# Two triangle-style layers on one core: Newton roots on VectorE, centring and normalising on GpSimd, the fourth contraction among residual steps

## The reference

```python
# layer 0
z_norm = _layer_norm(z, ln_w, ln_b)
a = (z_norm @ W_ap + b_ap) * jax.nn.sigmoid(z_norm @ W_ag + b_ag) * m
b = (z_norm @ W_bp + b_bp) * jax.nn.sigmoid(z_norm @ W_bg + b_bg) * m
out = jnp.einsum('bikc,bkjc->bijc', a, b)
return z + (out @ W_z + b_z)
# layer 1
x = _layernorm(pair_repr, ln1_w, ln1_b)
left = jax.nn.sigmoid(x @ left1) * (x @ left2)
right = jax.nn.sigmoid(x @ right1) * (x @ right2)
p = jnp.einsum('nsre,nkre->nske', left, right)
p = _layernorm(p, ln2_w, ln2_b)
g = jax.nn.sigmoid(jnp.einsum('nsrz,zy->nsry', x, gate))
q = jnp.einsum('nrse,ez->nsrz', p, out_w) * g
return residual + q
```

## Time and profile before

| | us |
|---|---|
| median of 3 runs | 1036.89 |
| lowest and highest | 1032.7, 1040.85 |
| the profiled execution | 1038.49 |
| its span in the trace | 1036.7 |
| mean granted TensorE clock (share of full speed) | 0.953 |

### The profile page before, as it was taken

How to read it: one execution, slowest core, us unless ns; L and a number is a source line. 1 busy time by engine, 2 the same in 40 slices (tenths; PEclk the granted TensorE clock), 3 DMA queues, 4 the chain that set the end, 5 groups by cost and what they waited for, 6 DMA issues and landing times.

```text
span 1036.7 us, 26385 instructions
## 1 busy us (share of the span) xinstructions
PE 832.8 (80%) x9820; PEld 794.4 (77%) x9820; DVE 763.3 (74%) x1851; ACT 635.2 (61%) x866; POOL 587.9 (57%) x409
## 2 busy tenths in 40 slices
PE   0744455576899899989579999998999899989875
PEld 0644445476899898979469999898989898989864
DVE  3799999976669967995592588825981698059796
ACT  0698877764757636753364476635763676256664
POOL 3599998885436604650582144423761467148797
PEclk9999986778999999999899999999999999999989
DMA  2355568998689817968683368874983598777665
GB/s 81 92 164 162 155 206 263 325 333 263 231 271 298 270 42 238 315 219 274 237 249 108 112 207 257 298 279 131 299 265 122 151 303 252 257 248 235 196 227 191
DMA packets 173238, 228.72 MB, mean 221 GB/s; under 512 B 11064, under 2 KB 109624, under 8 KB 171064
## 3 DMA queue, kind: packets, MB, share of 16 engines
q1 hardware_dynamic: 173112, 227.04, 69.2%
HBM read 134.73 MB, written 92.27 MB: 219 GB/s over the span
## 4 chain that ended last, share of the span: by engine, by line
PE 40%; DVE 21%; DMA 16%; issue 12%; ACT 4%; POOL 4%; SPq 3%; DVEq 0%; POOLq 0%; ACTq 0%
PE bank L1052 16%; PE bank L1032 7%; DVE stats L895 6%; DMA xin<-in_x_dram 6%; PE bank L1033 6%; PE ps_w L1082 5%; DVE split L939 4%; DMA chunk<-xcol 3%; DMA chunk<-xt 2%; DVE xc L932 2%; PE ps_t L1067 2%; DVE var L902 2%; DMA xt<-xt 2%; POOL rstd L633 2%; DVE xc L924 2%
## 5 line engine op out<-in xcount | busy, mean ns | idle before, releaser
L633 POOL TENSOR_TENSOR rstd<-var,minus_half 128x8 f32<-128x8 f32 x192 | 341.2, 1778 | 388.2 <-DVE var L902 388.2
L1052 PE MATMUL bank<-rhs,lhs 128*128 128x128 f32 x2048 | 246.7, 281 | 17.0 <-DVE lhs L875 9.2
L1052 PEld LDWEIGHTS bank<-rhs,lhs 128*128 128x128 f32 x2048 | 238.0, 196 | 20.6 <-DVE lhs L875 8.9
L689 ACT ACTIVATE sig<-bank 128x512 f32<-128x512 f32 x256 | 151.6, 601 | 72.2 <-PE bank L1033 69.3
L716 ACT ACTIVATE xt<-ps_x 128x1024 bf16<-128x1024 bf16 x128 | 130.9, 1023 | 61.9 <-PE ps_x L1093 45.9
L1093 PE MATMUL ps_x<-ident_b,split 128*128 128x128 bf16 x1024 | 85.6, 232 | 90.1 <-DVE split L939 89.6
L932 DVE TENSOR_TENSOR xc<-xc,rstd 128x504 f32<-128x504 f32 (+1 forms) x192 | 139.2, 725 | 23.0 <-POOL xc L647 19.8
L1093 PEld LDWEIGHTS ps_x<-ident_b,split 128*128 128x128 bf16 x1024 | 67.1, 103 | 103.0 <-DVE split L939 102.1
L1032 PE MATMUL bank<-w_rhs,chunk 128*128 128x128 bf16 x1024 | 135.2, 227 | 8.2 <-DVE rhs L867 3.3
L1032 PE MATMUL bank<-w_lhs,chunk 128*128 128x128 bf16 x928 | 131.4, 234 | 6.7 <-DVE lhs L867 4.4
L1082 PE MATMUL ps_w<-w_out,opair 128*128 128x128 f32 x896 | 124.2, 283 | 13.4 <-ACT opair L708 13.0
(11 more groups left out here) (97 smaller groups left out, 1441.6 us busy)
## 6 DMA issues: line engine op xcount, KB each, us to landing
chunk<-xt SPq DMA_DIRECT2D x90, 512.0 KB, 4.5
xt<-xt SPq DMA_DIRECT2D x80, 512.0 KB, 5.2
xin<-in_x_dram SPq DMA_DIRECT2D x128, 256.0 KB, 4.5
x<-xin SPq DMA_DIRECT2D x64, 256.0 KB, 5.0
xin<-x SPq DMA_DIRECT2D x64, 256.0 KB, 4.7
out_dram<-xin SPq DMA_DIRECT2D x64, 256.0 KB, 4.6
spill<-lhs SPq DMA_DIRECT2D x8, 1024.0 KB, 4.9
chunk<-xcol SPq DMA_DIRECT2D x16, 512.0 KB, 5.9
```

The lines of the kernel that those rows point to most:

```text
L633: g.tensor_tensor(rstd[:, m % 2], var[:, m % 2], minus_half[:, :], ALU.pow).then_inc(rooted, 1)
L689: a.activation(sig[:, s], v[:, 0:C, :], ACT.Sigmoid).then_inc(gated, 1)
L1052: last = mm(bank[:, n], operand["lhs"][:, kh, c, :], operand["rhs"][:, kh, c, :], start=kh == 0, stop=kh == HALVES - 1)
```

## The change

- **Roots.** `variance` and GpSimd's `root` go. For each pair of steps VectorE forms the inverse roots of 16 variances a partition by an integer guess and Newton's method in nine instructions, which `root_in_gap` places one by one between its other instructions. `stats` has four buffers. For z steps the roots are written to a PSUM tensor, for the others to SBUF. The factor 1.5 that the guess leaves out goes into the weights (`ROOT_FACTOR`).
- **Engines.** GpSimd centres all z and x steps and normalises all x and p steps; VectorE normalises the z steps and centres the p steps. GpSimd masks one half of the operands of contractions 1 and 2, beginning four ticks ahead of them; VectorE masks the other (512 elements a unit, one unit ahead).
- **Lags.** Centring and what follows run later: an x step centres at lag 5 (before: 4), its transpose at 7 (6), with steps every other tick at 8 and 10 (5, 7); z steps store at 5 (4), p steps at 5 (4), with their statistics at -2 (-1).
- **Fourth contraction.** The 16 ticks of x steps alone and the 16 of contraction 3 become 16 ticks with one x step and one unit each. The result of contraction 3 goes to the lhs operand's memory, and layer 1's first lhs half to `quad`; the w_out for these steps has its rows interleaved (`w_pairs`).
- **Start.** SyncE issues four x loads, then only the six loads of the first weight set; seven others at tick 1, the diagonal ones at tick 3; ScalarE issues ten. The other sets are prepared at ticks 7 to 9.

```diff
-Z_LAGS = dict(load=-2, stats=0, variance=0, root=0, centre=1, norm=1, high=1, low=2, turn_x=2, xt=3,
-              col=3, store=4, project=3, gates=4, make=5)
+Z_LAGS = dict(load=-2, stats=0, centre=1, norm=2, high=2, low=3, turn_x=3, xt=4,
+              col=4, store=5, project=4, gates=5, make=6)
+X_LAGS = dict(turn=0, turn_out=0, mix=1, load=1, add=2, keep=3, stats=3, centre=5,
+              norm=5, high=5, low=6, turn_x=7, xt=7, store=8, project=0, gates=0, make=1)
+P_LAGS = dict(stats=-2, centre=0, norm=1, turn=1, turn_out=2, mix=2, spread=-1,
+              gate=1, gate_out=3, scale=3, load=3, residual=4, store=5, gate_load=-3, project=0, gates=1, make=1)
...
     for n in range(STEPS):
-        tick("x alone", X_BASE + 2 * STEPS + n)
-    contraction(3)
+        tick("x in contraction", X_BASE + 2 * STEPS + n, unit=(3, n))
...
+NORM_EARLY, NORM_LATE = 0, 4 * STEPS
+OTHERS_AT = 7
...
 def centre_on_pool(m):
-    return m < Z_EARLY or Z_LATE <= m < P_BASE
+    return m < P_BASE
+
+def norm_on_pool(m):
+    return m < NORM_EARLY or m >= NORM_LATE
...
+        def roots_of(pair):
+            if OTHERS_AT + 5 <= 2 * pair and not norm_on_pool(2 * pair):
+                return ps_w[:, pair % 2, 0:2 * COLS].rearrange("p (s t) -> p s t", s=2)
+            return rstd[:, pair % 2]
...
-            for m in range(2):
+            for m in range(RING):
                 load_x(m)
-            for dst, src in loads:
-                sp.dma_start(dst, src).then_inc(loaded, 16)
+            for dst, src in first_loads:
+                sp.dma_start(dst, src).then_inc(first_loaded, 16)
...
             for t in range(T_END):
-                for m in due("centre", t):
-                    if centre_on_pool(m):
-                        centre(m)
+                for n in first_masks_at(t):
+                    mask_operand(n)
+                for m in due("centre", t, "zx"):
+                    centre(m)
                 for m in due("residual", t):
                     add_residual(m)
...
+                for m in due("norm", t):
+                    if norm_on_pool(m):
+                        normalise(m)
+                for q, u in later_masks_at(t):
+                    mask_later(q, u)
...
                 for c in range(0, COLS, 2):
...
+                    last = v.bn_stats(stats[:, m % 4, c:c + 2, :].rearrange("p a s -> p (a s)"), src)
+                    if c == COLS - 2:
+                        last.then_inc(stats_done, 1)
+                    root_in_gap()
...
+            def root(pair, n):
+                before = 8 * pair
+                if n == 0:
+                    dve.wait_ge(rooted, after(pair - 1))
+                    dve.wait_ge(stats_done, after(2 * pair + 1))
+                    v.tensor_scalar(minus_var[:, :, :], stats[:, 2 * (pair % 2):2 * (pair % 2) + 2, :, 2],
+                                    C * EPS, -0.5, ALU.add, ALU.mult).then_inc(newton, 1)
+                if n == 1:
+                    dve.wait_ge(newton, before + 1)
+                    v.tensor_scalar(guess[:, :, :].bitcast(I32), minus_var[:, :, :].bitcast(I32),
+                                    -0.5, GUESS, ALU.mult, ALU.add).then_inc(newton, 1)
+                if n in (2, 6):
+                    dve.wait_ge(newton, before + n)
+                    v.tensor_tensor(term[:, :, :], guess[:, :, :], guess[:, :, :], ALU.mult).then_inc(newton, 1)
+                if n == 3:
+                    dve.wait_ge(newton, before + 3)
+                    v.tensor_tensor(term[:, :, :], term[:, :, :], minus_var[:, :, :], ALU.mult).then_inc(newton, 1)
...
+                if n == 8:
+                    dve.wait_ge(newton, before + 8)
+                    dve.wait_ge(*normed_by(2 * pair - 3))
+                    v.scalar_tensor_tensor(roots_of(pair), term[:, :, :], 1.5, guess[:, :, :], ALU.add, ALU.mult
+                                           ).then_inc(rooted, 1)
```

478 lines of the change are left out of this document (290 added, 188 removed).

## The result

The changed kernel takes 1073.08 us (median; 1070.37 to 1076.9) where the kernel before takes 1036.72 (1032.7 to 1040.85) on the same chip: a ratio of 1.0353, 95% interval 1.0301 to 1.0405. It is slower by 36 us. The forecast was 1016 us, faster. VectorE is busy for 854.6 us (before: 763.3), GpSimd for 478.8 (587.9), TensorE for 851.0 (832.8).

The account below looks back on a forecast made before the run. VectorE was taken to bound the z steps, TensorE nearly full from 289 us on. Terms -12 + 5 + 3 + 0 + 3 - 5 - 17 + 0 - 4 + 5 = -22 from a 1036.7 span gave 1016 us; range 980 to 1056.

Parts of the forecast that it names:

- slot plus mean wait: Each small root instruction on VectorE: 0.085 slot plus 0.105 mean wait, 0.19 us, so 0.86 per step.
- A: Rival, slower: small root instructions meet GpSimd's work each time, z tick 4.5 us, x stages +13, total 1053; chance 0.23.
- the sum: Main forecast: VectorE's and TensorE's instruction times added per tick, with the mean wait; 1002 to 1026, chance 0.38.
- z steps, +8 forecast: z steps: +5 before masks, 0 under masks and from 147 to 212 us, +3 at hand-over to the products' second half.
- 0, at the price of +7 if that cover is gone: z steps from 147 to 212 us: DMA share of 0.88 covers VectorE's longer ticks, 0; without that cover +7.
- x steps with chunks, +3 forecast: Two x stages of 16 ticks: VectorE 4.06 a tick against 3.94 now, TensorE 3.99; +3 us.
- Contractions 1 and 2, -5 forecast: GpSimd takes half the masks ahead of time, bringing 37.90 us towards 35.70 without masks; -5 us for two.
- Merged contraction, -17 forecast: Fourth contraction among the residual steps: 88.70 us becomes 71.9, at 4.1 a tick after 12.5 us for the first x load; -17.
- Rival C's ring of x buffers: Merged ticks paced by the four x buffers at 4.9, +11, half the early weights' gain lost, +3: 1030; chance 0.17.
- p steps with chunks, -4 forecast: Two p stages: VectorE 4.06 a tick against 4.16 now, GpSimd's normalising wait hidden by the lags; -4 us.
- Last p steps, +5 forecast: Last p steps alone: 3.30 us a step of work that cannot overlap, against 3.0 now; +5 us over 16.
- Start, -12 forecast: Early weights: first product about 22.5 us, 18 earlier, other weights' work moved behind it; -12, bounds -8 and -17.

Follow-up runs that it names:

- Experiment 1: Changed kernel with the first Newton tensor (minus_var) of z pairs in PSUM instead of SBUF: 1051.54 us, ratio 1.0157 to the kernel before.
- Experiment 4: Changed kernel with GpSimd's 48 masks of contraction 0 over 8 elements instead of 512: 1039.48 us, ratio 1.004 to the kernel before.
- Experiment 5: Changed kernel with seven of the nine root instructions replaced by 16-element bn_stats, output not the reference's: 1015.5 us, ratio 0.9814 to the kernel before.
- experiment 3: Changed kernel with seven of the nine root instructions left out, output not the reference's: 986.13 us, ratio 0.9507 to the kernel before.
- experiment 12: Kernel before with merged fourth contraction and early weights, TensorE's transposes ahead of the unit as before: 1006.51 us, ratio 0.9704 to the kernel before.
- experiment 8: Kernel before with merged fourth contraction, early weights and the change's TensorE order (transposes behind the unit): 1011.05 us, ratio 0.9774 to the kernel before.
- experiment 10: Changed kernel with the masks of contractions 1 and 2 wholly on VectorE: 1065.04 us, ratio 1.0282 to the kernel before.
- Experiment 2: Changed kernel with the fourth contraction taken out of the x steps again: 1095.08 us, ratio 1.0554 to the kernel before.
- experiment 6: Kernel before with only the merged fourth contraction and the change's TensorE order in ticks with a unit: 1025.14 us, ratio 0.9897 to the kernel before.
- experiment 11: Changed kernel with the p steps normalised on VectorE instead of GpSimd: 1069.97 us, ratio 1.0313 to the kernel before.
- experiment 7: Changed kernel with the small loads issued late, as in the kernel before: 1083.96 us, ratio 1.0467 to the kernel before.

## Why the prediction was wrong

**The step that failed: the mean wait of a small instruction.** "I take slot plus mean wait, 0.085 + 0.105 = 0.19." The 0.105 came from `variance`, one instruction a step in one fixed place. It measured how often that place met GpSimd, not how often nine places would, and even that as an average of two opposite cases. In the kernel before, `variance` over the 16 z ticks ahead of the masks, then over the first x stage (count, min/median/max ns, first and last start):

```profile
L902 DVE TENSOR_TENSOR var<-stats,c_eps x16: 157/615/620, 41.4 to 89.1; 128x8 f32<-128x8 f32 x16
L902 DVE TENSOR_TENSOR var<-stats,c_eps x14: 155/164/174, 298.1 to 352.3; 128x8 f32<-128x8 f32 x14
```

Half of the former take 615 ns or more, the longest of the latter 174. The nine stand before and after the large instructions, and GpSimd's centring starts 0.1 to 0.2 us after `low` ends, with the mask chained to it: 2.3 us of GpSimd's work in a row, which the next two or three root instructions meet on every pair. Their slots came to 0.265 on the mean. The 0.075 more, times 864, is 65 us of VectorE's time, three times the forecast gain; the prediction itself named 0.04 us as the point from which A decides. Experiments 1, 4 and 5 show the hold from three sides (operand, other engine, other instruction): 21.5, 33.6 and 58 us. The slot of 0.085 was not the mistake, though the row it came from has 8 elements and not 16: unheld ones are 0.07 to 0.10 us apart in the timelines above. Nor was the addition of the stages, except that it started from the profiled execution; from the median of 1036.9 it gives 1015.

**The number cost as well.** Experiment 5 against 3 gives 29 us for 672 instructions that nothing holds. The forecast had put their unhindered slots in the ticks' sums but let them be hidden where the sum stayed below the old tick: 0 under masks, 0 behind them, -4 in the p steps. With seven of the nine left out the z steps from product 0 to 64 take 234.2 us, 14 less than before, and with them unheld 252.5, 4 more.

**z steps, +8 forecast with the hand-over's 3, +26 measured** (32.0 in the four z stages, less the 6 booked against the early weights). The first stage came nearly as forecast, +12.5 against 5 and the 6, with small instructions of 0.25 us; the miss begins where GpSimd's masks do, with 0.42 and 0.44. Rival A's hand-laid pair, 9.1 us, was closer than the sum's 6.92: 8.46 measured. The sum used a mean where the hand sequence was there, worked out in the same text. "0, at the price of +7 if that cover is gone" for 147 to 212 us came as +5.1: the DMA share is 0.81 there, no longer 0.88, and VectorE is busy for 69.17 of 70.50 us.

**x steps with chunks, +3 forecast, +3.4 measured.** Right, and A's +13 wrong: a small instruction takes 0.26 us there, as `variance` did on the mean. The sum of 4.06 a tick stands against 4.11 and 3.93. But VectorE is busy for only 58.57 us of the first stage's 65.80, 3.66 a tick, so it is not full as the sum has it, and part of the agreement is luck. Without seven of the nine the two stages are only 5.7 us shorter, 3.84 a tick, where the sum had put TensorE at 3.99.

**Contractions 1 and 2, -5 forecast, +8.8 measured.** Two things were missed. TensorE's order (transposes behind the unit) isn't in the forecast at all; it costs 3 us in each by experiment 12 against 8. The split masks cost about 1 each, and another 1 each in the stage ahead (experiment 10). These and the small instructions are not additive: experiment 3, which has the order and the split masks and few small instructions, takes 38.9 and 37.1, 1 more than before in each.

**Merged contraction, -17 forecast, -21.8 measured.** The mechanism was right: the first x add comes 12.4 us after contraction 2 and still waits for its load,

```profile
527.81 0.69 DVE L1046 TENSOR_TENSOR xin<-xin,ps_w 128x512 f32<-128x512 f32 x1 [16.93 <-DMA xin<-in_x_dram]
```

but the units do not wait with it; they run from 515.5 to 577.0 us, 3.84 a unit tick, which is TensorE's sum of 3.87 rather than the 4.1 taken. Rival C's ring of x buffers did not pace them. What the forecast lacked is the stage behind: +4.2 instead of 0, since the last x steps of the merged stage end in it. Experiment 2 undoes that (23.9 us for its first quarter instead of 27.4) and experiment 6, without Newton, has it too.

**p steps with chunks, -4 forecast, +15 measured.** Here too the small instructions meet GpSimd (0.36 and 0.37 us on the mean). Its residual and normalising run one behind the other, and two root instructions fall on them; VectorE's timeline, then GpSimd's:

```profile
753.67 0.88 DVE L1014 TENSOR_TENSOR term<-guess 128x16 f32<-128x16 f32 x1
754.48 0.68 DVE L1070 TENSOR_TENSOR xc<-lhs,stats 128x512 f32<-128x512 f32 x1
755.09 1.01 DVE L1017 TENSOR_TENSOR term<-term,minus_var 128x16 f32<-128x16 f32 x1
```

```profile
753.22 1.30 POOL L729 TENSOR_TENSOR xin<-xin,split 128x512 f32<-128x512 f32 x1 [5.30 <-DMA xin<-x]
754.48 1.58 POOL L722 TENSOR_TENSOR xc<-xc,rstd 128x512 f32<-128x512 f32 x1
```

L1014 ends at 754.55, the residual at 754.52; L1017 ends at 756.10, the normalising at 756.06. The hold goes both ways in these rows: the normalising itself took 1.58 us, with a mean of 1.10 over all of them, while VectorE's centring L1070 ran. Experiment 5 takes the hold away and has 67.1 and 66.9; experiment 11 takes the normalising out of GpSimd's queue and has 73.5 twice. So "normalising on GpSimd delays TensorE's turns in the p stages" was not it.

**Last p steps, +5 forecast, +11.5 measured.** The last 64 bn_stats of the change,

```profile
L992 DVE BATCH_NORM_STATS2 stats<-quad x64: 271/281/296, 999.4 to 1050.9; 128x6 f32<-128x128 f32 x64
```

take 51.5 us from first to last start, 4.3 more than in the earlier trace rows: the forecast's step. The other 7 stand around them: from the last one to the end 20.2 us pass, 13.5 before. With seven of the nine left out it is still 18.3, so 5 of the 7 don't come from those seven. The longer lags (statistics at -2, store at 5: two ticks more) are the likely cause, not shown by a run; the forecast had counted them as cover and never as a tail.

**Start, -12 forecast, 11 and 14 measured** (experiments 7 and 8). First product at 23.3, forecast 22.5.

Of the rivals A was the one that came, priced too low: 1053 against 1073. Its excess over the sum was put at 37 us, in z and x steps; it came to 57, in z and p steps and the contractions. The whole lies beyond the range, which ended at 1056, since the p stages' +15 and the contractions' +8.8 were in no case. The rows from which A's tick was laid out were there; the sum should have gone by them, and the mean of `variance` been kept as the lower bound.

The Trainium skill's "SBUF — State Buffer", section Who interferes with whom, says that the pair of ports which VectorE and GpSimd share is held by one instruction for its whole length, whichever came first, and that a VectorE instruction with two SBUF inputs wants it. The trace agrees for L1017 and L1014 (0.61 and 0.88 us for 16 elements). By the same section a VectorE instruction with one SBUF input contends only in a 2-port mode; L1006, with one input and its output in SBUF, was held for 0.94 us, and with its output in PSUM took 0.18. That would fit if it ran in such a mode, which no row shows. The prediction had weighed the same rule and taken the mean all the same.

**Still open.** Whether the lags make the 5 us tail at the end, and which, was not tried. The granted clock of TensorE is lower in the first two z stages of the change than before (0.81 and 0.65 against 1.00 and 0.91; in the third 0.76 against 0.71); since VectorE is busy for 66.98 of 68.10 us in the second, it is not needed to explain the time, but no run separates it. Experiment 10's 8 us are explained to little over a half.

## What to carry to other kernels

A small VectorE instruction with its operands in SBUF costs its 0.08 us only where it misses GpSimd's tile-wide work; where it meets a centring, mask, residual or normalising of 1.0 to 1.6 us, it costs the rest of that, 0.6 to 1.2 us in the timelines here. Before moving work to many small instructions, lay one tick of both engines out by hand and count the places that GpSimd's chain covers; the mean of one instruction in one place does not carry over to nine. If such work must stay, put one operand in PSUM or shorten the GpSimd instruction beside it, and look for where the wait goes next. And test the parts of a change apart: two of these parts alone, with the old order on TensorE, make the kernel 3% faster, the whole makes it 3.5% slower.
